# Attention: the projection of values, from behind the first run of score units to the middle of the second

## The reference

```python
q = (x @ Wq).reshape(B, N, H, Dh).transpose(0, 2, 1, 3)
kv = x @ Wkv                      # k is the first half of its columns, v the second
s = jnp.einsum('bhid,bhjd->bhij', q * scale, k)
gm = jnp.max(s, axis=-1, keepdims=True)          # over all keys, masked ones too
p = jnp.where(causal_mask, 0.0, jnp.exp(s - gm))
out = jnp.einsum('bhij,bhjd->bhid', p, v) / (jnp.sum(p, axis=-1, keepdims=True) + EPS)
x = x + out.transpose(0, 2, 1, 3).reshape(B, N, H * Dh) @ Wo + bo
```

## Time and profile before

| | |
|---|---|
| median of 3 runs | 2098.7 us (2096.18 to 2099.93) |
| the profiled execution's own time | 2101.55 us |
| its span, first to last instruction | 2099.6 us |
| busy: PE, DVE, POOL, ACT | 1835.9, 1683.0, 1346.3, 956.1 us |
| attention, from its first value unit on | 48.6 us to about 1310 us of the span |
| value units | 32, from 48.61 us to 1221.35 us |

### The profile page before, as it was taken

The page is one execution under the profiler, slowest core; times in us unless marked ns, Lnnn a source line. Parts: engine busy times, 40 slices in busy tenths (PEclk is TensorE's granted clock), DMA queues, the critical chain, the costliest instruction groups (busy, mean ns, idle before and its releaser), DMA issues. The chain is left out here.

```text
span 2099.6 us, 35185 instructions
## 1 busy us (share of the span) xinstructions
PE 1835.9 (87%) x11743; PEld 1283.3 (61%) x11743; DVE 1683.0 (80%) x2683; ACT 956.1 (46%) x1920; POOL 1346.3 (64%) x1156
## 2 busy tenths in 40 slices
PE   2999999999999999999999998579974776666997
PEld 1666766666666666676666665458853333345885
DVE  4888888888888888888888886678874887967886
ACT  3344444444444444444444443347864323234885
POOL 2467657657667667667667668169972766714997
PEclk9999999999999999999999999589985989957998
DMA  2000000000000000000000000100000000000001
GB/s 81 1 1 1 2 1 1 1 1 2 1 1 1 1 1 1 1 1 1 1 1 1 2 1 1 41 31 21 30 0 26 21 20 19 2 1 31 21 30 40
DMA packets 22102, 23.20 MB, mean 11 GB/s; under 512 B 1296, under 2 KB 15440, under 8 KB 21968
## 3 DMA queue, kind: packets, MB, share of 16 engines
q1 hardware_dynamic: 21968, 21.40, 3.1%
HBM read 6.72 MB, written 2.10 MB: 4 GB/s over the span
## 5 line engine op out<-in xcount | busy, mean ns | idle before, releaser
L866 DVE TENSOR_REDUCE attn_neg<-attn_shared 128x2 f32<-128x1024 f32 x512 | 618.3, 1225 | 172.9 <-PE attn_shared L990 171.5
L806 ACT ACTIVATE attn_prob<-attn_shared 128x1024 f32<-128x1024 f32 (+3 forms) x384 | 311.0, 812 | 411.2 <-PE attn_shared L1018 411.2
L768 POOL TENSOR_TENSOR attn_row_sum<-attn_row_sum,attn_prob 128x1024 f32<-128x1024 f32 (+3 forms) x256 | 418.7, 1636 | 24.2
L481 ACT ACTIVATE experts_weighed<-experts_y,experts_gate 128x128 f32<-128x128 f32 x1024 | 278.1, 382 | 112.0 <-PE experts_y L570 108.6
L508 DVE SCALAR_TENSOR_TENSOR experts_acc<-experts_y,experts_gate,experts_acc 128x128 f32<-128x128 f32 x960 | 268.6, 344 | 43.4 <-PE experts_y L570 33.2
L763 POOL TENSOR_TENSOR attn_row_sum<-attn_prob 128x1024 f32<-128x1024 f32 x64 | 135.5, 2118 | 222.6 <-ACT attn_prob L806 220.1
L1035 PE MATMUL attn_pv<-attn_prob,attn_v 128*64 128x512 f32 (+3 forms) x1536 | 267.5, 490 | 1.2 <-POOL attn_prob L745 1.2
L568 PE MATMUL experts_y<-kept_w_hi,experts_xs_hi 128*128 128x512 f32 x512 | 201.2, 393 | 45.2 <-DMA experts_xs_lo<-kept_xT_lo 45.2
L986 PE MATMUL attn_shared<-attn_qk_hi 64*128 64x512 f32 x1024 | 223.0, 424 | 4.1 <-DVE attn_qk_lo L884 2.4
L890 DVE RECIPROCAL attn_den<-attn_den 128x256 f32<-128x256 f32 x128 | 214.6, 1718 | 12.1 <-ACT attn_den L829 12.1
L745 POOL TENSOR_TENSOR attn_prob<-attn_prob,attn_below 128x256 f32<-128x256 f32 x256 | 187.4, 732 | 49.6 <-ACT attn_prob L806 45.6
(11 more groups left out here) (192 smaller groups left out, 3558.2 us busy)
## 6 DMA issues: line engine op xcount, KB each, us to landing
experts_xs_hi<-kept_xT_hi SPq DMA_DIRECT2D x16, 256.0 KB, 2.3
experts_xs_lo<-kept_xT_lo SPq DMA_DIRECT2D x16, 256.0 KB, 2.4
kept_x<-in_L_attn_a_x_dram SPq DMA_DIRECT2D x4, 512.0 KB, 6.2
norm_f_w_raw<-_ffn_expert_weights_dram SPq DMA_DIRECT2D x4, 512.0 KB, 6.1
linear_xs_hi<-kept_xT_hi SPq DMA_DIRECT2D x8, 256.0 KB, 2.3
linear_xs_lo<-kept_xT_lo SPq DMA_DIRECT2D x8, 256.0 KB, 2.4
out_dram<-kept_x SPq DMA_DIRECT2D x4, 512.0 KB, 5.4
attn_prob<-in_L_attn_a_Wkv_dram SPq DMA_DIRECT2D x2, 512.0 KB, 5.5
```

The lines of the kernel that those rows point to most:

```text
L481: ins = act.activation(weighed[n][:, e, :], y[(2 * quad + odd) % BANKS][:, e * D:(e + 1) * D], ACT.Copy, scale=g)
L768: pool.tensor_tensor(row_sum[n][:, :, at:], row_sum[n][:, :, at:], src[:, :, at:], ALU.add).then_inc(add_ok, 1)
L806: act.activation(prob[n % RING][:, :, at:], buffer((p, i))[:, :, at:], ACT.Exp).then_inc(exp_ok, 1)
L866: dve.tensor_reduce(neg[p % 2][:, :, b, half], buffer((p, b, half))[:, :, :], AX.X, ALU.max, negate=True).then_inc(max_ok, 1)
```

## The change

The value unit leaves the tail of stage 0. In the code it stands now in the middle of stage 1, between s3 and s4, on PE, on ACT (behind the exponential of the third turned unit of the stage) and in the rotation of buffers. Nothing is added and nothing is left out.

```diff
     for r in range(FIRST, LAST):
-        shared += row_order(r, 0)
+        shared += row_order(r, 0, 0) + row_order(r, 0, 1) + row_order(r, 1, 0)
         if value_unit(r):
             shared.append(("value", *value_unit(r)))
-        shared += row_order(r, 1)
+        shared += row_order(r, 1, 1)
...
                 for t in range(STEPS):
-                    for p, i in turned_units(r, t):
+                    for p, i in turned_units(r, t)[:3]:
+                        exponential(p, i)
+                    if t == 1 and value_unit(r):
+                        values(*value_unit(r))
+                    for p, i in turned_units(r, t)[3:]:
                         exponential(p, i)
                     if t == 0:
                         if valid(r - 1):
                             product_out(r - 1, 1)
                         if valid(r):
                             rows(r, 1)
-                        if value_unit(r):
-                            values(*value_unit(r))
                         if valid(r - 1):
                             denominator(r - 1, 1)
...
             for r in range(FIRST, LAST):
-                row_stage(r, 0)
+                row_stage(r, 0, 0)
+                row_stage(r, 0, 1)
                 if valid(r - 1):
                     for i in range(8, 12):
                         product(r - 1, i)
                 if valid(r):
                     turned(r, 1)
-                if value_unit(r):
-                    values(*value_unit(r))
                 if valid(r - 1):
                     sums(r - 1, 1)
                 if valid(r):
                     for i in range(0, 3):
                         product(r, i)
 
-                row_stage(r, 1)
+                row_stage(r, 1, 0)
+                if value_unit(r):
+                    values(*value_unit(r))
+                row_stage(r, 1, 1)
```

More of the change, by code:

```diff
@@ L616, in turned_units, with row_order @@
         return [(p, i) for i in range(6 * t, 6 * t + 6)] if valid(p) else []
-    def row_order(r, t):
+    def row_order(r, t, m):
         s, st = score_units(r + 1, t), turned_units(r, t)
-        return [u for n in range(4) for u in (*s[n:n + 1], *st[n:n + 1][:n < 3])] + \
-               [u for n in range(4) for u in (*s[4 + n:5 + n], *st[3 + n:4 + n][:n < 3])]
+        return [u for n in range(4) for u in (*s[4 * m + n:4 * m + n + 1], *st[3 * m + n:3 * m + n + 1][:n < 3])]
     def score_index(p, b, half):
@@ L1055, in outwards, with row_stage @@
                 ins.then_inc(out_ok, 1)
-            def row_stage(r, t):
+            def row_stage(r, t, m):
                 s, st = score_units(r + 1, t), turned_units(r, t)
[L1059 to L1064, removed]
+                for n in range(4):
+                    if s:
+                        scores(*s[4 * m + n])
+                    if st and n < 3:
+                        shifted(*st[3 * m + n])
             for r in range(FIRST, LAST):
-                row_stage(r, 0)
+                row_stage(r, 0, 0)
+                row_stage(r, 0, 1)
                 if valid(r - 1):
```

## The result

The changed kernel takes 2130.68 us, median of 5 runs (2129.48 to 2133.55); the kernel before took 2099.93 beside it (2096.18 to 2101.92). The ratio is 1.0151, with a 95% interval of 1.0140 to 1.0162: it is slower, by 1.5%. The profiled executions are 2131.29 and 2101.55 us, 29.7 apart, at a granted clock of 0.941 in both. The last `sums` of the attention starts 29.5 us later than before (1338.64 against 1309.14), so nearly all of it arises in the attention.

A forecast was written before the change was run, and what follows sets the result against it. PE was taken as the bound, ending last nearly everywhere. 29 rounds at 0.85 us, about 0.4 in round 0 and 0.5 in round -1 made 25.6 us, giving 2124 us against the median 2098.7; range 2108 to 2132.

The forecast's parts named there:

- The tail gives back 0.65 us, not 1.58: Tail of stage 0: without the unit's 1.58 us, `sums` waits for ACT's copy of the rows, so 0.65 us is gained.
- The unit costs 1.79 us at the new place: Between s3 and s4 on PE: 1.49 us for the unit, 0.10 and 0.20 for changes of matmul shape going in and out.
- The walk of stage 1: PE's starts followed from s3 to the transposes: 0.29 us comes back in waits, the round is 0.85 us longer.
- cheap unit: Rival, stage 1: shape changes are hidden, 0.45 us in each of 30 rounds and 0.5, +14 us, 2113; chance 0.14.
- filled waits: Rival, stage 1: the unit fills PE's waits, each round 0.26 us shorter, -8 us, 2091; chance 0.07.
- Rounds -1 and 0: Start of the attention: 0.5 us for round -1 as PE's lead over DVE goes, about 0.4 for round 0.
- The sum, 25.6 us: Whole attention: 24.7 us from 29 rounds, plus about 0.4 in round 0 and 0.5 in round -1.
- the round of 0.85: Rounds 1 to 29: each 0.85 us longer, together 24.7 us.
- DVE at the end: Rival, end of the round: DVE slides 0.3 us further than PE in half the rounds, 4.5 us more, 2129; chance 0.08.
- The median: Profiled execution before lay 2.9 us above the median of the runs, so 2127.1 became 2124.
- The likeliest case alone: Forecast case without its rivals: 0.7 to 1.0 us a round, 2119 to 2129 us; chance 0.66.

The follow-up runs named there:

- reordered tail: Changed kernel with `turned` ahead of the product in the tail, and ACT's copy of the rows ahead of its copy of the product: 2113.27 us, ratio 1.0056.
- the reorder: Kernel before, value unit still in the tail, with `turned` and ACT's copy of the rows moved ahead of the product: 2106.78 us, ratio 1.0024.
- the earlier `low`: Changed kernel with DVE's `low(r + 2, 0)` between the two reciprocals of stage 1 instead of behind both: 2131.00 us, ratio 1.0144.

## Why the prediction was right, and where it fell short

- *The tail gives back 0.65 us, not 1.58.* Right, shown by the unit left out and by the one behind `sums`. The wait by name came as forecast, 21.3 us in 31 times; first product to `sums` was forecast at 3.64 and is 3.65.
- *The unit costs 1.79 us at the new place.* Right to 0.05: it is 1.84. Going in cost 0.14 us (s3 to the unit is 0.84 instead of 0.70) and a second row at 0.22 (658.35, then 658.57) instead of 0.12, coming out 0.21 and 0.33 (659.74, 659.95, and 660.28 for the next pair) instead of 0.12 and 0.23. s3 to s4 is 2.44 us, forecast 2.38.
- *The walk of stage 1.* From s3 on, forecast and measured: 384-column unit +3.19 and +3.24, s5 +3.89 and +3.93, 256-column unit +4.68 and +4.72, 128-column unit +6.10 and +6.11, transposes +7.43 and +7.45. Before it was 5.93 to the transposes, so 0.32 of the 1.84 us came back in waits where I had 0.29. The rival "cheap unit" is out with this, and so is "filled waits": DVE idles for 1.27 us before s4, and PE waits anew at the 256- and the 128-column unit.
- *Rounds -1 and 0.* Forecast 0.5 us for round -1; there DVE's eight maxima of stage 1 take 9.65 us (67.90 to 77.55) instead of 9.14, with one idle time of 0.42 among them. Up to the end of round 0 the lag is 1.1 us, forecast 0.9, and with the 28.4 of the later rounds that makes the 29.5. The 1.1 are less sure than the rest: kernels with the same work up to round 0 start it at times that differ by several tenths of a microsecond between their traces.
- *The sum, 25.6 us.* Too small: the profiled executions are 29.7 apart. The term that was too small is the round of 0.85, taken as the same 29 times. It is 0.88 in 14 rounds and 1.07 in 15, which gives 28.4 instead of 24.7. I had this in the rival "DVE at the end" (0.3 us in half of the rounds, 4.5 us in all), as an alternative to the forecast. It was an addition to it: DVE slides by 0.25 us, and 0.2 of it reach PE in 15 rounds. The earlier trace rows said that DVE has no idle time there, which should have been enough to put it into the sum. I also looked for the slide in the wrong place, in when DVE's maxima end; they end with PE, as before. What it came from is how long DVE's small operations last.
- *The median.* I took off 2.9 us because the profiled execution of before lay that much above its median. That of after lies 0.6 above its own. This is scatter between runs, 2.2 us of the 6.4 by which 2124.3 missed; the other 4.1 are the sum.
- Of the experiments' expectations three sizes were off: 0.17 us of changes of shape in the unit behind `sums`, DVE's hold on the reordered tail (0.2 instead of 0.6), and the 0.2 us that the reorder costs in the kernel before. Of the 3 us that the earlier `low` was to bring, the trace shows 1.9.

The range held the time, near its upper end. The likeliest case alone, 2119 to 2129 us, did not: it was the rival at the end of the round that had set the upper bound. No kernel that I tried and that does all the work beats the one before. The nearest is the reorder on the kernel before, 0.24% slower.

## What to carry to other kernels

What a unit gives back where it leaves is not its own time but its time less the latency that it covered: look in the trace for a round that has no such unit (here the last two), and read the wait that stands in its place. At the new place it costs its own time, and more where its matmuls have another shape than their neighbours. A trace in which an engine has no idle time in some of the rounds says that these rounds have to be summed apart, not as a rival case.

## What the runs showed of the hardware

Short operations of DVE can last many times their own length beside POOL. `least`, 128x8, in the trace after (shortest, median and longest of 64, in ns):

```profile
L875 DVE TENSOR_TENSOR attn_least<-attn_neg x64: 166/919/2369, 67.4 to 1306.8; 128x8 f32<-128x8 f32 x64
```

In that trace 41 of the 64 last over 0.3 us, and each of these ends 0.02 us behind the end of a POOL operation that had begun before it; the other 23 last 166 to 169 ns, and none of them began while a POOL operation was already under way. The same holds for 62 of the 64 casts behind them, which end 0.03 us behind POOL's. The Trainium skill has a rule for it ("SBUF — State Buffer", "SBUF: two separate sides"): VectorE and GpSimd share a pair of ports as an exclusive lock, and the one that comes second waits out the other's whole instruction; it holds for a VectorE operation with two inputs in SBUF against a GpSimd operation that reads SBUF. The rows of `least`, which has two such inputs, agree. The cast has one, and waited in the same way; whether it runs in one of the modes that the Trainium skill names beside this no run here shows.

Between pairs of 64-row matmuls and full ones PE lost time at both changes, 0.24 us going in and 0.20 coming out in the changed kernel, and the unit behind `sums` (next to matmuls of 64 columns) cost 1.75 us instead of 1.58. At the end of stage 1, coming out into the transposes cost nothing (0.12 us, the pace).
